# Node and edge transposes placed one by one between the projection matmuls of a three-layer graph kernel

## What is computed

```python
def layer(h, adj, Wl, bl, Ws, bs, Wr, br, g, beta):
    u = einsum('bid,bjd->bij', h, h) / sqrt(384)
    delta = softmax(u) * adj
    attn = delta / (delta.sum(-1, keepdims=True) + 1e-10)
    hl, hs, hr = h @ Wl.T + bl, h @ Ws.T + bs, h @ Wr.T + br
    ctx = upper(attn) @ hl + diag(attn)[..., None] * hs + lower(attn) @ hr
    return relu((ctx - mean(ctx)) / sqrt(var(ctx) + 1e-12) * g + beta)

h = relu(layernorm(x));  x = x + layer(layer(h, ..., params0), ..., params1)
h = relu(layernorm(x));  x = x + layer(h, ..., params2)
```

## Time and profile before

| | |
|---|---|
| median of 3 runs | 1339.25 us (1338.05 to 1341.2) |
| profiled execution, first to last instruction | 1338.4 us; the profile gives no other time of its own for it |
| TensorE matmul busy | 1301.0 us (97%), 7818 instructions |
| TensorE weight loads busy | 1269.7 us (95%) |
| VectorE busy | 1271.9 us (95%) |
| ScalarE busy | 803.3 us (60%) |
| POOL busy | 879.6 us (66%) |
| mean granted TensorE clock | 0.996 |

### The profile page before, as it was taken

How to read it: one execution, slowest core, us unless ns; L and a number is a source line. 1 busy time by engine, 2 the same in 40 slices (tenths; PEclk the granted TensorE clock), 3 DMA queues, 4 the chain that set the end, 5 groups by cost and what they waited for, 6 DMA issues and landing times.

```text
span 1338.4 us, 29377 instructions
## 1 busy us (share of the span) xinstructions
PE 1301.0 (97%) x7818; PEld 1269.7 (95%) x7818; DVE 1271.9 (95%) x3308; ACT 803.3 (60%) x1949; POOL 879.6 (66%) x918
## 2 busy tenths in 40 slices
PE   8999999999999899999999999999999999999996
PEld 6999999999999899999999999999999999999996
DVE  7999999999999799999999999999999999999998
ACT  6666666666666555555555555566666566566663
POOL 3766666666667566666665666776776776767675
PEclk9999999999999999999999999999999999999999
DMA  5110111111011211011110110211101010101111
GB/s 170 33 47 31 47 34 45 38 40 47 31 54 32 74 48 32 31 47 31 41 38 31 47 31 32 77 50 41 39 31 47 31 47 31 47 31 44 34 45 39
DMA packets 46229, 59.20 MB, mean 44 GB/s; under 512 B 3696, under 2 KB 46192, under 8 KB 46192
## 3 DMA queue, kind: packets, MB, share of 16 engines
q1 hardware_dynamic: 46192, 58.77, 13.8%
HBM read 46.17 MB, written 12.58 MB: 44 GB/s over the span
## 4 chain that ended last, share of the span: by engine, by line
PE 62%; DVE 18%; issue 12%; POOL 3%; ACT 2%; DMA 1%; DVEq 1%; SPq 0%; ACTq 0%; POOLq 0%
PE right_bank L400 15%; PE left_bank L400 15%; PE self_bank L400 14%; PE context_bank L434 10%; DVE side_rows L708 5%; PE score_bank L374 4%; DVE context L744 3%; PE node_bank L363 3%; POOL rstd L864 2%; DVE rows L757 1%; DVE score L642 1%; DVE context L714 1%; DMA vector_rows<-vectors 1%; DVE stats L718 1%; ACT node_t L494 1%
## 5 line engine op out<-in xcount | busy, mean ns | idle before, releaser
L868 POOL TENSOR_TENSOR side_parts<-side_rows,side_parts 128x384 fp32r<-128x384 f32 x384 | 426.1, 1120 | 175.8 <-ACT side_parts L534 172.6
L400 PE MATMUL self_bank<-weight,node_t 128*128 128x384 f32 x1728 | 339.9, 340 | 0.6 <-POOL weight L887 0.4
L400 PE MATMUL right_bank<-weight,node_t 128*128 128x384 f32 x1728 | 333.2, 336 | 5.5 <-DVE side_rows L708 5.3
L400 PE MATMUL left_bank<-weight,node_t 128*128 128x384 f32 x1728 | 332.1, 335 | 0.7 <-DVE weight L693 0.7
L534 ACT ACTIVATE side_parts<-side_rows 128x384 fp32r<-128x384 f32 x384 | 191.2, 522 | 224.9 <-DVE side_rows L708 155.0
L400 PEld LDWEIGHTS right_bank<-weight,node_t 128*128 128x128 f32 x1728 | 301.5, 188 | 10.5 <-issue 9.8
L400 PEld LDWEIGHTS self_bank<-weight,node_t 128*128 128x128 f32 x1728 | 298.1, 188 | 1.0 <-issue 0.6
L400 PEld LDWEIGHTS left_bank<-weight,node_t 128*128 128x128 f32 x1728 | 298.1, 188 | 1.0 <-issue 1.0
L875 POOL TENSOR_TENSOR context<-self_rows,context 128x384 f32<-128x384 f32 x192 | 195.5, 1018 | 120.5 <-ACT context L549 118.3
L434 PE MATMUL context_bank<-side_parts,attn_t 128*128 128x384 f32 x1152 | 248.4, 350 | 16.3 <-issue 15.8
L434 PEld LDWEIGHTS context_bank<-side_parts,attn_t 128*128 128x128 f32 x1152 | 192.2, 188 | 22.2 <-issue 21.3
(11 more groups left out here) (56 smaller groups left out, 1726.3 us busy)
## 6 DMA issues: line engine op xcount, KB each, us to landing
rows<-x SPq DMA_DIRECT2D x32, 384.0 KB, 3.4
adj_in<-adj SPq DMA_DIRECT2D x96, 128.0 KB, 2.1
io<-x SPq DMA_DIRECT2D x32, 384.0 KB, 3.1
out<-io SPq DMA_DIRECT2D x31, 384.0 KB, 2.5
piece<-weights SPq DMA_DIRECT2D x18, 192.0 KB, 2.9
vector_rows<-vectors SPq DMA_DIRECT2D x15, 192.0 KB, 4.6
rows<-weights SPq DMA_DIRECT2D x3, 576.0 KB, 7.0
out<-io SPq DMA_DIRECT2D x2, 192.0 KB, 1.9
```

The lines of the kernel that those rows point to most:

```text
L400: mm = nc.tensor.matmul(bank[:, 0:D], node_t[:, s.parity, k, c, a], weight[:, s.phase % 2, w, c, b], start=(c == 0 and a == b), stop=last)
L868: nc.gpsimd.tensor_tensor(side_parts[:, side, LO], side_rows[:, side], side_parts[:, side, HI].bitcast(F32), ALU.subtract).then_inc(side_l ...
```

## The change

The waits of both transposes become functions of their own (`nodes_ready`, `edges_ready`), and `transpose_nodes` and `transpose_edges` now make one transpose per call. `project` takes the tile whose nodes are to be turned, or a flag for the edges. A node transpose follows each of the second, fifth and eighth matmul of the nine; edge transposes follow the first, second, fourth and fifth. `project_side` and `project_self` wait for what the transposes need before the first matmul. The node transposes of tile 0 of the next step go into left(0), those of tile 1 into self(0), the edge transposes into right(1).

```diff
-            def transpose_nodes(s, k):
+            def nodes_ready(s, k):
                 pe.wait_ge(source_ready, s.tile(k) + 1)
                 at_least(pe, node_lo, s.tile(k) - 1)
-                for c in range(CH):
-                    mm = nc.tensor.transpose(node_bank[k][:, c * P:(c + 1) * P], source[:, k, c * P:(c + 1) * P], ident)
-                mm.then_inc(node_moved, 1)
+            def transpose_nodes(s, k, c):
+                mm = nc.tensor.transpose(node_bank[k][:, c * P:(c + 1) * P], source[:, k, c * P:(c + 1) * P], ident)
+                if c == CH - 1:
+                    mm.then_inc(node_moved, 1)
...
-            def transpose_edges(s):
+            def edges_ready(s):
                 pe.wait_ge(blocks_placed, 2 * s.n + 2)
                 pe.wait_ge(attn_lo, s.n)
-                for k in range(2):
-                    for ul in range(2):
-                        at = (2 * k + ul) * P
-                        mm = nc.tensor.transpose(edge_bank[:, at:at + P], edge_block[:, k, ul], ident)
-                mm.then_inc(edges_moved, 1)
-
-            def project(s, k, w, bank, done):
+            def transpose_edges(s, k, ul):
+                at = (2 * k + ul) * P
+                mm = nc.tensor.transpose(edge_bank[:, at:at + P], edge_block[:, k, ul], ident)
+                if (k, ul) == (1, 1):
+                    mm.then_inc(edges_moved, 1)
+
+            def project(s, k, w, bank, done, turned=None, edges=False):
                 for c in range(CH):
                     for a, b in ((HI, HI), (HI, LO), (LO, HI)):
...
+                        if (c, a) == (CH - 1, LO):
+                            mm.then_inc(done, 1)
+                        if turned is not None and (a, b) == (HI, LO):
+                            transpose_nodes(*turned, c)
+                        if edges and c < 2 and a == HI:
+                            transpose_edges(s, c, b)
...
                 weights_split(s, k, side)
-                project(s, k, side, side_bank[side], side_product[side])
+                if turned is not None:
+                    nodes_ready(*turned)
+                if edges:
+                    edges_ready(s)
+                project(s, k, side, side_bank[side], side_product[side], turned, edges)
...
             def body(s):
                 prev, nxt = s.ahead(-1), s.ahead(1)
                 project_side(s, 0, RIGHT)
-                project_side(s, 0, LEFT)
-                if nxt.exists():
-                    transpose_nodes(nxt, 0)
+                project_side(s, 0, LEFT, turned=(nxt, 0) if nxt.exists() else None)
                 if prev.exists():
                     weigh(prev, 1)
-                if nxt.exists():
-                    transpose_nodes(nxt, 1)
-                project_self(s, 0)
-                project_side(s, 1, RIGHT)
-                if not s.bounded:
-                    transpose_edges(s)
+                project_self(s, 0, turned=(nxt, 1) if nxt.exists() else None)
+                project_side(s, 1, RIGHT, edges=not s.bounded)
                 if nxt.exists():
                     scores(nxt)
```

More of the change, by code:

```diff
@@ L384, in turn_cross @@
                 mm.then_inc(cross_turned, 1)
-            def transpose_edges(s):
+            def edges_ready(s):
                 pe.wait_ge(blocks_placed, 2 * s.n + 2)
                 pe.wait_ge(attn_lo, s.n)
-                for k in range(2):
-                    for ul in range(2):
-                        at = (2 * k + ul) * P
-                        mm = nc.tensor.transpose(edge_bank[:, at:at + P], edge_block[:, k, ul], ident)
-                mm.then_inc(edges_moved, 1)
-            def project(s, k, w, bank, done):
+            def transpose_edges(s, k, ul):
[4 more added lines that the diff above has]
+            def project(s, k, w, bank, done, turned=None, edges=False):
                 for c in range(CH):
                     for a, b in ((HI, HI), (HI, LO), (LO, HI)):
-                        last = (c, a) == (CH - 1, LO)
                         mm = nc.tensor.matmul(bank[:, 0:D], node_t[:, s.parity, k, c, a], weight[:, s.phase % 2, w, c, b],
-                                              start=(c == 0 and a == b), stop=last)
-                mm.then_inc(done, 1)
+                                              start=(c == 0 and a == b), stop=(c, a) == (CH - 1, LO))
+                        if (c, a) == (CH - 1, LO):
[4 more added lines that the diff above has]
+                            transpose_edges(s, c, b)
             def weights_split(s, k, w):
@@ L410, in weights_split, with project_side @@
                         pe.wait_ge(piece_lo, (s.phase - 1) * PIECES + (w + 1) * CH)
-            def project_side(s, k, side):
+            def project_side(s, k, side, turned=None, edges=False):
                 pe.wait_ge(node_hi, s.tile(k) + 1)
@@ L416, in project_side, with project_self @@
                 weights_split(s, k, side)
-                project(s, k, side, side_bank[side], side_product[side])
-            def project_self(s, k):
+                if turned is not None:
[3 more added lines that the diff above has]
+                project(s, k, side, side_bank[side], side_product[side], turned, edges)
+            def project_self(s, k, turned=None):
                 at_least(pe, self_scaled, s.tile(k))
                 weights_split(s, k, SELF)
-                project(s, k, SELF, self_bank, self_product)
+                if turned is not None:
+                    nodes_ready(*turned)
+                project(s, k, SELF, self_bank, self_product, turned)
             def weigh(s, k):
@@ L469, in _ @@
             start = Step(0, 0, 0)
-            transpose_nodes(start, 0)
-            transpose_nodes(start, 1)
+            for k in range(2):
+                nodes_ready(start, k)
+                for c in range(CH):
+                    transpose_nodes(start, k, c)
             keep_busy(1)
```

## The result

The changed kernel takes 1395.59 us (median of 4 runs, 1391.97 to 1397.43) against 1338.65 us for the kernel before on the same chip: ratio 1.0418, 95% interval 1.0398 to 1.0437, so 4.2% slower. The forecast was 1382, its range 1365 to 1400. The profiled execution spans 1392.9 us, 54.5 more than before; the prediction's sum was 42.7.

The account below looks back on a forecast made before the run. TensorE and VectorE, both over 95% busy, were taken to bound the kernel by handing work to each other. Phase terms 8.5 + 27 + 7.2 = 42.7 us over the 1338.4 us span gave 1381.1, median 1382; range 1365 to 1400.

Parts of the forecast that it names:

- rival (b): More waits: VectorE gates some phase 1 steps, or a single transpose costs 150 ns; +15 us, 1397 us; chance 0.14.
- 125 ns: Forecast price of one transpose between 384-column matmuls on TensorE, taken from the turn_cross pair; 0.05 us more per step.
- (c): Weight loads on TensorE hide behind each other, a transpose costs 58 ns; +3.3 us, 1343 us; chance 0.04.
- (d): Not slower: transposes nearly free through hidden loads, deciding at 52 ns; 1332 us at 40 ns; chance 0.02.
- Phase 0, +8.5: Late second transpose group delays VectorE's split and so C (weigh); 0.27 to 0.28 us a step, 31 steps, +8.5 us.
- rival (a): VectorE's gates in phases 0 and 2 don't form because its 3.60 us stretch shrinks; about 1368 us; chance 0.12.
- Phase 1, +27: right(1) waits for the placed blocks, TensorE idle 1.32 us a step; steps 14.97 against 14.08 us, 30 steps, +27 us.
- Phase 2, +7.2: left(0) waits for the source copy, delaying VectorE's second split 0.45 us in short steps; 14 pairs and three end steps, +7.2 us.

Follow-up runs that it names:

- e4: Changed kernel with all transposes still single but earlier in their projections, each wait directly ahead of the first transpose it is for; 1338.08 us, ratio 1.0005.
- e3: Kernel before with only tile 1's row of three node transposes moved behind the eighth matmul of self(0), waits unmoved; 1347.24 us, ratio 1.0071.
- e9: Kernel before with only tile 1's row of node transposes moved behind the fifth matmul of self(0), waits unmoved; 1337.96 us, ratio 1.0001.
- e7: Kernel before, transposes still in rows, tile 1's row behind self(0)'s eighth matmul, waits ahead of left(0), self(0) and right(1); 1390.69 us, ratio 1.0401.
- e6: Changed kernel with all transposes in place and each wait moved directly ahead of the first transpose it is for; 1376.53 us, ratio 1.0291.
- e2: Changed kernel with only the edge transposes interleaved, their wait ahead of right(1), node transposes back in rows; 1366.93 us, ratio 1.0209.
- e5: Changed kernel with only tile 0's node transposes interleaved in left(0), source wait ahead of it, the other transposes back in rows; 1346.48 us, ratio 1.0056.

## Why the prediction was right, and where it was off

Direction, mechanism and place were right; the size was 12 us short by the profiled spans, inside the range. That 1395.59 is near the 1397 of rival (b) is chance: a transpose didn't cost 150 ns, and in phase 1 VectorE waited for TensorE.

- *A transpose by itself costs what one in a row does.* Right, and my 125 ns was too high: 117 ns in the changed kernel, and e4 shows no cost at all. The rivals (c) and (d), hidden loads, are out. The sentence of the Trainium skill on weight loads pulled ahead ("TensorE: Matmul & The Clock Gate", "Step-by-step: what each phase is for") was weighed as the way to 58 ns per transpose. It holds here for one load ahead and no more, as the earlier trace rows had it: 117 ns, in the changed kernel as in a row. None of the 7818 weight loads of its profile starts before the matmul ahead of its own.
- *Phase 0, +8.5.* Measured 8.6. C starts 4.29 us behind right(1), forecast 4.22. e3 shows it with the late row alone, e9 the threshold. VectorE's stretch stayed (3.64 for 3.60), so rival (a) didn't happen. That the sum is so close is luck in part: the gate costs 0.29 us a step instead of 0.22, the six transposes about 0.01 instead of 0.05.
- *Phase 1, +27.* Measured 35.8; this term was mis-sized. The step was forecast at 14.97 and is 15.17. I had counted 0.10 us from the placed blocks to TensorE, from a row in which the edge transposes waited. It is 0.25, with two instructions with waits behind the one for the blocks (under e7); 0.04 more is in the way over ScalarE. The instruction behind the first matmul starts 0.25 later instead of 0.17, and singles at 117 instead of 125 ns take these 0.08 back. Over 28 steps the whole is 31.6 us. The other 4 us are in the last two steps, which I had put at 0.90 each like the rest: they take 33.2 instead of 29.2.
- *Phase 2, +7.2.* Measured 10.2. Short steps went up by 0.60, not 0.45. The source wait was there, 0.30 us for 0.23; the rest lies between left(0) and VectorE's second split, which starts 7.37 us behind right(0) instead of 6.79. Of the 0.60, e6 gets 0.35 back by moving the waits, e3 shows 0.21 for the late transposes alone. The count was off too: behind the first two steps there are 13 pairs, not 14, and the last three steps, put at 0.30 each, cost 0.71 each (41.8 us for 39.7).
- *The sum of the parts.* Alone, the late row costs 0.7%, the edge wait 2.1%, left(0) 0.6%, which makes 3.4%; all three in the changed kernel cost 4.2%. The remaining 0.8%, 11 us, is one interaction: with the node transposes early, right(1) waits less (14.73 us a step in e2, 15.17 with both), since the wait then starts from VectorE's bias and not from the last transpose. Over 28 steps the 0.44 us are 12 us.

## What to carry to other kernels

Moving a wait ahead of a group of matmuls puts the whole group behind it: put the wait directly ahead of the instruction that needs it, and ask what the group had been covering. Where one instruction has several waits, look in the queue as built for the one that comes last, and see that it stands behind the others, which isn't always so when it is written last: each instruction with a wait behind it costs about 0.1 us here. A producer's place in a queue has a threshold, not a slope: find the reader's own earliest time, and up to there the place is free. Where each small matmul exposes one weight load of the next, spreading them out changes nothing, as e4 shows here; count exposed loads before reordering.

## What the runs showed of the hardware that I had not expected

TensorE's clock fell inside a kernel that is busy 94% of the time. In the last-but-one step of phase 1 right(1) waits 1.97 us by the bracket, where it is 1.34 in a middle step. ScalarE's side copy, ahead of the blocks, has waited 2.67 us for VectorE's bias there. That ends 6.63 us behind right(0), where it is 5.58 in a middle step, and VectorE's queue has the input statistics of the third layer (L632) in it too; how much each piece of work costs isn't separated. Right behind the wait the granted clock of a 5 us stretch is 0.66, a mix of the full 2.4 GHz and of 1.2:

```profile
911.00:916.00 5.00, 5.00 (x26) 4.98 (x24) 2.66 (x8) 2.37 (x5) 2.13 (x4) 0.66 0.00 0
```

```profile
909.90 0.42 PE L406 MATMUL right_bank<-weight,node_t 128*128 128x384 f32 x1 [1.97 <-ACT edge_block L531]
...
912.51 1.48 PE L378 MATMUL score_bank<-node_t 128*128 128x256 f32 x6
913.79 2.20 PE L406 MATMUL left_bank<-weight,node_t 128*128 128x384 f32 x9
```

The six score matmuls take 1.28 us from start to start instead of 0.71 and left(1) 2.04 instead of 1.57: about 1 us in these two groups. The spread of the runs goes with it: the changed kernel's fastest run, 1391.97 us, has a mean granted clock of 0.998, its slowest, 1397.43 us, 0.993. The start of phase 1 is such a place in the kernel before as well (right(1) waits 2.31 us there, until 443.83, and the granted clock of 443.83 to 449.00 is 0.67). Of the twelve profiles that of e2 has the longest wait there: right(1) waits 4.26 us for the blocks and the granted clock of the step is 0.83:

```profile
435.31:455.85 20.54, 16.28 (x86) 15.61 (x86) 12.06 (x30) 8.22 (x25) 9.66 (x10) 0.83 0.20 56
```

A long wait isn't always followed by a lower clock. In e5's profile right(1) waits 2.47 us at the start of phase 1 and the granted clock of the 5 us behind it (444.00 to 449.00) is 1.00. In e6's an edge transpose waits 1.17 us there, and the granted clock of 451.00 to 456.00 is 0.66. What decides it isn't shown by these runs.
